# Down projection of a transformer block on one Trainium2 core: plain fp32 product or three split products

## The reference, cut to what matters

```python
c  = attention(x)                          # (8, 128, 512), summed over 8 groups of heads
s  = silu(c @ w_gate.T)                    # (8, 128, 1376)
s  = where(|s| is among the 688 smallest of its row, 0, s)
h  = s * (c @ w_up.T)
x1 = x + h @ w_down.T                      # the down product: 1376 -> 512
y  = x1 @ weight[adapter_ids[b]].T
out = x1 + (y @ unpack_int4(packed_w).T * scale_w + bias)
```

## Time and profile before

| | |
|---|---|
| median of 3 runs | 1397.92 us (1397.61 to 1399.25) |
| the profiled execution, its own time | 1399.51 us |
| its span (first to last instruction) | 1397.7 us |
| PE busy | 1376.4 us (98%) |
| DVE busy | 1181.5 us (85%) |
| ACT busy | 880.4 us (63%) |
| POOL busy | 795.0 us (57%) |
| granted TensorE clock, mean | 0.996 |

### The profile page before, as it was taken

One profiled execution on the slowest core, in us unless ns is written; L12 is line 12 of the kernel. 1 busy time (PEld: TensorE's weight loads), 2 busy tenths in 40 slices (PEclk: granted clock), 3 DMA queues, 4 the chain that ended last, 5 costly groups with the idle time before them and its releaser, 6 DMA issues.

```text
span 1397.7 us, 22868 instructions
## 1 busy us (share of the span) xinstructions
PE 1376.4 (98%) x7762; PEld 1159.6 (83%) x7762; DVE 1181.5 (85%) x2580; ACT 880.4 (63%) x2236; POOL 795.0 (57%) x832
## 2 busy tenths in 40 slices
PE   8899999999999999999999999999999999999998
PEld 6788888888888888888888888888888786667766
DVE  8989898989898989898989898999899887766662
ACT  6677676767676767676767676767777742222221
POOL 6867666666666666666676666666666500221211
PEclk9899999999999999999999999999999999999999
DMA  6111211111121112111211121212121203211121
GB/s 229 58 31 32 75 62 31 56 51 61 33 75 34 60 33 75 33 62 32 73 36 61 31 76 31 61 31 72 31 72 32 103 20 124 72 46 46 48 64 49
DMA packets 27408, 80.42 MB, mean 58 GB/s; under 512 B 9522, under 2 KB 10546, under 8 KB 23954
## 3 DMA queue, kind: packets, MB, share of 16 engines
q1 hardware_dynamic: 10898, 45.29, 9.2%
q0 software_dynamic: 16384, 33.59, 8.1%
HBM read 76.74 MB, written 2.10 MB: 56 GB/s over the span
## 4 chain that ended last, share of the span: by engine, by line
PE 89%; DVE 7%; issue 2%; ACT 2%; another core or an unknown queue 0%; POOL 0%; ACTq 0%; DVEq 0%
PE proj_ps L110 9%; PE proj_ps L112 9%; PE proj_ps L111 9%; PE turn_ps L750 9%; PE score_ps L112 5%; PE value_ps L110 5%; PE value_ps L111 5%; PE value_ps L112 5%; PE score_ps L111 5%; PE score_ps L110 5%; PE out_ps L932 5%; PE gu_ps L112 3%; PE gu_ps L110 3%; PE gu_ps L111 3%; PE turn_ps L712 2%; PE turn_ps L719 2%
## 5 line engine op out<-in xcount | busy, mean ns | idle before, releaser
L521 POOL DMA_INDIRECT kg<-kc,idx x256 | 260.7, 1018 | 277.9 <-issue 263.2
L1193 ACT ACTIVATE probs<-probs,shift,rstd 128x640 f32<-128x640 f32 x256 | 234.5, 918 | 137.3 <-DVE shift L1544 135.0
L531 POOL DMA_INDIRECT vg<-vc,idx x256 | 259.0, 1012 | 70.7 <-issue 70.7
L1580 DVE TENSOR_TENSOR pt_lo<-turn_ps,pt_hi 128x512 fp32r<-128x512 f32 x320 | 217.2, 686 | 44.6 <-ACT pt_hi L1199 39.1
L1555 DVE CUSTOM_DVE_ANT_0 probs<-score_ps,mask 128x640 f32<-128x640 f32 x256 | 208.7, 821 | 38.8 <-PE score_ps L112 35.6
L1199 ACT ACTIVATE pt_hi<-turn_ps 128x512 fp32r<-128x512 f32 x320 | 186.4, 593 | 86.6 <-PE turn_ps L750 77.4
L750 PE MATMUL turn_ps<-cst,probs 128*128 128x128 f32 x1280 | 192.7, 273 | 1.7 <-DVE qt_lo L1532 0.9
L110 PE MATMUL proj_ps<-w_hi,xt_parts 128*128 128x256 f32 (+1 forms) x500 | 190.4, 381 | 1.4 <-issue 1.4
L750 PEld LDWEIGHTS turn_ps<-cst,probs 128*128 128x128 f32 x1280 | 158.0, 141 | 28.5 <-DVE probs L1573 2.3
L112 PE MATMUL proj_ps<-w_hi,xt_parts 128*128 128x256 f32 (+1 forms) x500 | 169.6, 339 | 0.0
L111 PE MATMUL proj_ps<-w_lo,xt_parts 128*128 128x256 f32 (+1 forms) x500 | 168.6, 337 | 0.0
(11 more groups left out here) (214 smaller groups left out, 3213.5 us busy)
## 6 DMA issues: line engine op xcount, KB each, us to landing
w_raw<-wqkv SPq DMA_DIRECT2D x7, 1536.0 KB
wo_raw<-wo SPq DMA_DIRECT2D x8, 1024.0 KB
wa_sb<-wa SPq DMA_DIRECT2D x7, 1024.0 KB, 4.8
kg<-kc,idx POOLq DMA_INDIRECT x256
vg<-vc,idx POOLq DMA_INDIRECT x256
wg_raw<-wg SPq DMA_DIRECT2D x2, 1376.0 KB
wu_raw<-wu SPq DMA_DIRECT2D x1, 2752.0 KB
wd_sb<-wd SPq DMA_DIRECT2D x1, 2560.0 KB, 9.7
```

The source lines that it names most:

```text
L521: pool.indirect_dma_start(kg[:, b % 2, c, :], None, kc, bass.IndirectOffsetOnAxis(ap=idx[:, s // B % 2, b * NC + c:b * NC + c + 1], axis=0))\
L531: pool.indirect_dma_start(vg[:, b % 2, c, :], None, vc, bass.IndirectOffsetOnAxis(ap=idx[:, s // B % 2, b * NC + c:b * NC + c + 1], axis=0))\
L1193: act.activation(row, row, ACT.Exp, bias=shift[:, h:h + 1], scale=rstd[:, b % 2, h:h + 1], accum_out=sums[:, h:h + 1])\
L1580: dve.tensor_tensor(pt_lo[:, at, :], turn_ps[1 - j % 2][:, :], pt_hi[:, at, :].bitcast(F32), ALU.subtract).then_inc(p_lo_done[j], 1)
```

## The change

The down product becomes three split products. Its weights are split once for all tiles, and h is split in each tile:

- The down weights are loaded before the last step of phase 1 ends (all but the last chunk). ACT rounds them (`split_wd`, `split_wd_end`), DVE subtracts. The high parts of chunks 4 to 9 have a tile of their own (`wd_hi_own`); those of chunks 0 to 3 and of the last one lie in rows 0 to 4 of `acc` (`wd_hi_acc`), which are free once `front` has transposed those attention results. So tile 0 splits only chunks 4 to 9, tile 1 chunks 0 to 9, and tiles 2 to 7 all 11; the rest stays plain.
- ACT's `copy_h` now writes the rounded `ht_hi`, and DVE has a new operation `split_h(i, n)` for each job, which reads PSUM and `ht_hi` and writes `ht_lo`. PE waits for it through `h_ready`: `turn_h(i, 2)` may overwrite the PSUM of job 0 only after `split_h(i, 0)`, and the down product starts only after `split_h(i, 0)` and `split_h(i, 1)`.
- The selection works in place: one `m_sb` and one `w_sb` in place of two each, `junk` inside `w_sb`, and h written over s. So `magnitudes(i)` waits for h of tile i-1.
- `front` loses the copy `c_sb`: ACT rounds straight from PSUM, and the subtraction goes from POOL to DVE (`split_c`).
- The output is summed in `y` and not in `acc`; `copy_y` waits for the output transfer of the tile before.

```diff
+                    def split_down(i, c):
+                        return i >= (1 if c < 4 else 2 if c == NF - 1 else 0)
...
                     def turn_h(i, n):
...
-                            wait(pe, h_copied[0], i + 1)
+                            h_ready(i, 0)
...
+                    def h_ready(i, n):
+                        if n == 0:
+                            wait(pe, h_copied[0], 1)
+                        wait(pe, h_lo_done, 3 * i + n)
+                        if n == 2 and not split_down(i, NF - 1):
+                            wait(pe, h_copied[2], i + 1)
...
-                            last = pe.matmul(out_ps[:, :], ht[0:width, c, :], wd_sb[0:width, c, :],
-                                             start=(c == 0), stop=(c == NF - 1))
+                            if c == 0:
+                                h_ready(i, 0)
+                                h_ready(i, 1)
+                            elif c == 8:
+                                h_ready(i, 2)
...
+                            if split_down(i, c):
+                                last = product3(pe, to, (ht_his[t][0:width, c, :], ht_los[t][0:width, c, :]), (hi, lo),
+                                                first, end)
+                            else:
+                                last = pe.matmul(to, ht_raw[0:width, c, :], raw, start=first, stop=end)
...
                     def magnitudes(i):
                         wait(act, silu_done, i + 1)
-                        act.activation(m_sb[i % 2][:, :], s_sb[i % 2][:, :], ACT.Abs, accum_out=sum_m[i % 2][:, :])\
+                        wait(act, h_done, i)
+                        act.activation(m_sb[:, :], s_sb[i % 2][:, :], ACT.Abs, accum_out=sum_m[i % 2][:, :])\
                             .then_inc(abs_done, 1)
...
                     def pick(i):
-                        for guess in range(len(STEP_SIZES)):
-                            pick_guess(i, guess)
+                        pick_guess(i, 0)
+                        if i > 2 and i + 1 < B:
+                            split_c(i + 1)
+                        pick_guess(i, 1)
+                        pick_guess(i, 2)
+                        if i == 2:
+                            split_h(1, 0)
+                            split_wd(2)
+                            split_h(1, 1)
+                            split_h(1, 2)
+                        if i == 3:
+                            split_wd_end()
                         pick_near(i)
+                        if i > 2:
+                            split_h(i - 1, 0)
                         pick_edge(i)
+                        if i > 2:
+                            split_h(i - 1, 1)
+                            split_h(i - 1, 2)
...
                     pick_edge(0)
+                    split_wd(1)
                     drop_lower_half(0)
+                    split_wd(0)
+                    split_h(0, 1)
+                    split_h(0, 2)
                     unpack(1)
                     unpack_bias()
                     for i in range(1, B):
                         pick(i)
                         times_up(i)
+                        if i == 1:
+                            split_c(3)
                         drop_lower_half(i)
+                    for n in ALL_JOBS:
+                        split_h(B - 1, n)
```

More of the change, by code:

```diff
@@ new lines, in down_products @@
+                    def down_products(i, to, cols):
+                        t = own(i)
+                        for c in range(NF):
+                            width, first, end = FCH[c][1], c == 0, c == NF - 1
+                            raw, hi, lo = (w[0:width, cols] for w in wd_places(c))
+                            if c == 0:
[3 more added lines that the diff above has]
+                                h_ready(i, 2)
+                            if i == 0 and c in (4, 8):
+                                pe.wait_ge(wd_lo_done, 1 if c == 4 else 2)
+                            elif i == 1 and first:
+                                pe.wait_ge(wd_lo_done, 3)
+                            elif i == 2 and end:
+                                pe.wait_ge(wd_lo_done, 4)
+                            if split_down(i, c):
[3 more added lines that the diff above has]
+                                last = pe.matmul(to, ht_raw[0:width, c, :], raw, start=first, stop=end)
+                        last.then_inc(downed, 1)
@@ L1361, in copy_h @@
                         full = sum(width == P for _, width in job)
-                        last = act.activation(hts[t][:, c:c + full, :].rearrange("p c t -> p (c t)"),
+                        into = ht_his[t] if split_down(i, c) else ht_raw
+                        last = act.activation(into[:, c:c + full, :].rearrange("p c t -> p (c t)"),
                                               to[:, 0:full * P], ACT.Copy)
-                        for m in range(full, len(job)):
-                            width = job[m][1]
-                            last = act.activation(hts[t][0:width, c + m, :], to[0:width, m * P:(m + 1) * P], ACT.Copy)
+                        if full < len(job):
+                            width = job[full][1]
+                            into = ht_his[t] if split_down(i, c + full) else ht_raw
+                            last = act.activation(into[0:width, c + full, :], to[0:width, full * P:(full + 1) * P],
+                                                  ACT.Copy)
                         last.then_inc(h_copied[n], 1)
@@ new lines, in split_h @@
+                    def split_h(i, n):
+                        t = own(i)
+                        job, c, to = HT_JOBS[n], 4 * n, h_ps(i, n)
+                        dve.wait_ge(h_copied[n], i + 1)
+                        full = sum(width == P for _, width in job)
+                        last = dve.tensor_tensor(ht_los[t][:, c:c + full, :].rearrange("p c t -> p (c t)"),
+                                                 to[:, 0:full * P],
+                                                 ht_his[t][:, c:c + full, :].rearrange("p c t -> p (c t)").bitcast(F32),
+                                                 ALU.subtract)
+                        if full < len(job) and split_down(i, c + full):
+                            width = job[full][1]
+                            last = dve.tensor_tensor(ht_los[t][0:width, c + full, :],
+                                                     to[0:width, full * P:(full + 1) * P],
+                                                     ht_his[t][0:width, c + full, :].bitcast(F32), ALU.subtract)
+                        last.then_inc(h_lo_done, 1)
```

213 lines of the change are left out of this document (124 added, 89 removed).

## The result

| | median us | runs | ratio to before | clock |
|---|---|---|---|---|
| before | 1398.45 | 4, 1397.61 to 1399.25 | | 0.996 (profiled run) |
| changed | 1417.26 | 4, 1413.49 to 1418.07 | 1.0129 [1.0109, 1.0149] | 0.988 to 0.993 |

A forecast was written before the change was run, and what follows sets the result against it. PE, busy 98% of the span, was taken to set the pace. Waits of 22.2 and 0.7 us against 13.5 saved gave +9.5; five clock falls added 9.5: +19 on 1397.92, so 1417, range 1405 to 1423.

The forecast's parts named there:

- What the product saves: Down products in phase 2: 9.45 us plain, 7.62 split, so 1.83 less per full tile and 13.5 in all.
- The quarter: Down product: three products for four passes would save 2.36 of 9.45 us; the prediction went by the rows' 1.83 instead.
- When DVE is ready: Tile steps 4 to 6, T being the first up product's start: PE wants h's low part at T+14.1, starts at T+17.15.
- pick(2) starts: Tile step 2 on DVE: the pick starts near 1193.1 instead of 1189.6, behind subtractions and the magnitudes of tile 2.
- the working of step 2: Tile step 2: PE waits 3.3 us at the third group of transposes, down saves 1.65, net +1.65.
- The sum without the clock: All tile steps and the end part: 22.2 us of waits and 0.7 against 13.5 saved, +9.5 us.
- where -0.4 stood: Tile step 1: split_h(0, 1) delays the down product by 0.6 us against 1.0 saved.
- The step that failed: DVE's added split_c: taken as hidden behind POOL's addition in tile steps 4 to 6, costing nothing, at worst 0.65 us.
- The clock: New PE waits in phase 2: the clock falls to half behind five of six, +9.5 us; 64% for falls at most waits.
- a sign of being wrong: Phase 2: the prediction is wrong if the clock stays at 1.00 in spite of waits above 2.4 us.
- the 1.9 us taken from phase 1: Price of one clock fall: half of a 3.9 us slow stretch seen after a 2.43 us gap in phase 1.
- One row was misread: The page before the change: TensorE's granted clock read as full in all but two of 40 slices.

The follow-up runs named there:

- plain_down: The changed kernel with the old fp32 down product, no DVE split of weights or h, the rest of the change kept: 1401.20 us, ratio 1.0017.
- no_low: The changed kernel without DVE's subtractions of h; the third matmul of each chunk reads h's high part instead: 1389.11 us, ratio 0.9930.
- split_early: The changed kernel with DVE's subtractions for jobs 1 and 2 moved inside pick_edge in picks 3 to 7: 1396.99 us, ratio 0.9985.
- gate_twice: The changed kernel with useless repeated matmuls on PE before the down products of tile steps 3 to 7: 1410.60 us, ratio 1.0082.

## Why the prediction was right, and where it was not

**What the product saves: right.** Tile steps 4 to 6 go from 32.48 us (plain_down) to 30.65 (no_low), 1.83 each, as worked out from the pitch of 0.231 us. The quarter, an estimate from the four passes that the Trainium skill gives for true fp32 (FP8 and Floating Point Precision, TensorE Precision Notes), would have been 2.36; no run here shows it, and the measurement decides.

**When DVE is ready: right to 0.1 us in tile step 4 (T+17.12, T+17.15 forecast).** PE waits 2.84 us in steps 4 to 6 (3.05 forecast), 3.19 in step 3 (3.7 and 0.2), and 5.64 in step 7, of which 0.45 stood before as the wait for ACT; 5.2 more were forecast. In step 2 it waits 0.97 for POOL and 2.19 for `ht_lo`, together 3.16 (3.3). split_early shows that in steps 3 to 6 this is place alone, no_low that it is DVE's low part alone.

pick(2) starts at 1193.10, as forecast (1193.1), but that is luck: phase 1 of this execution was 0.9 us shorter than in the profile of before (silu(1) starts at 1154.72 and not at 1155.66). Counted from silu(1), pick(1) starts 1.8 us later (2.0 forecast), and pick(2) 4.4 (3.5 forecast). From the start of pick(1) to the end of h of tile 1 DVE takes 21.9 us and not 20.6, which the prediction had unchanged. Half of this is `split_c(3)` (0.68 us, its row stands under plain_c_late), which the working of step 2 leaves out. The other half is a meeting with POOL, in order of time on the two engines:

```profile
1177.33 2.31 DVE L1963 SCALAR_TENSOR_TENSOR w_sb<-m_sb,edge 128x1376 f32<-128x1376 f32 x1
```

```profile
1176.89 1.29 POOL L593 TENSOR_TENSOR x<-x,xn_sb 128x512 f32<-128x512 f32 x1 [44.39 <-ACT x L1417]
1178.27 2.52 POOL L598 TENSOR_TENSOR xn_sb<-x,bias 128x512 f32<-128x512 f32 x1
```

The pass takes 1.65 us elsewhere. Here POOL's addition was there first, and the pass became 0.66 longer; it then held POOL's next addition up.

**The sum without the clock: 9.5 forecast, about 10.5 measured.** From gate_twice less before, by the table, with the one fall of its last part (1.6) taken off: step 2 +2.24 (forecast 1.65), step 3 +2.40 (2.1), steps 4 to 6 +1.28 each (1.25), from silu(7) to the end +1.8 (2.4). The profiled execution of before had 0.8 us more span than the median of its runs (1397.7 against 1396.9), so what comes before silu(2) is nearer +0.2 than -0.6, where -0.4 stood. The terms that were too small are those up to step 2, by about 1.2 us. The step that failed is the one that took moved work at nothing: 1.3 us more on DVE between pick(1) and h of tile 1, as above, with PE waiting for what comes behind it. The prediction had seen that DVE and POOL hold each other up, but costed it and `split_c` only in tile step 4. (plain_down's +2.5 is not the price of this: in the changed kernel `split_c(3)` doesn't wait for ACT, and behind the 0.97 us for POOL PE would wait for `ht_lo` anyway.)

**The clock: right in kind, 9.5 forecast, about 8.3 measured.** 6.7 us are shown by the medians of gate_twice, 1.6 are the fall left in its profile. The Trainium skill (TensorE: Matmul & The Clock Gate, HAM oscillation) would have every portion behind a wait begin cold; the trace agrees in four of six waits of this execution, with two of 2.84 us at full clock and a third of 2.84 at half. The prediction had named a clock that stays full behind more than 2.4 us as a sign of being wrong, and twice it did. Each fall was also cheaper than the 1.9 us taken from phase 1: 1.6 in step 2 (36.26 against 34.70), 0.8 in step 3 (35.64 against 34.86), 1.3 in step 5 (35.01 against 33.72, where 35.5 to 36.5 was forecast), 1.3 in step 7 (8.95 us for the down product, 7.62 at full clock). In phase 1 PE had further gaps while it ran slowly, here products follow without one; that this makes the difference is not shown. These four are 5.0 us, in the shortest of the executions; those with clock 0.988 are some 4.6 us longer, about what two or three more falls and longer ones cost.

One row was misread: of the 40 slices of the earlier trace rows one, not two, is below 9. Nothing hangs on it.

So 1417.0 against 1417.26 is closer than the steps deserve: 1.0 us too little waiting and 1.2 us too much clock cancel. What carried the forecast was the order of time on two engines.

## What to carry to other kernels

When a product gets cheaper by a new operand, find the place of that operand in the queue of the engine that makes it, and compare its end with the time at which PE now wants it; 28 us of difference (1417.3 to 1389.1) hung on that, and 20 of them, the clock's part included, on moving two instructions ahead of search passes that PE was not waiting for. A buffer that is saved by working in place ties an engine's next pass to the reader of the last one, and holds what stands behind it in that queue; put what others wait for ahead of it. Remove a wait and read the trace again: the next one was there already, 3 us behind.

## What the runs showed of the hardware

- The clock behind an idle stretch of PE is not settled by its length alone: of three waits of 2.84 us at the same place of a tile step, two left it at 1.00 and one brought it to 0.51. A wait of 2.2 us in tile step 2 lowered it in one of four profiled executions.
- Useless matmuls in place of waits made the kernel 6.7 us faster (1417.26 to 1410.60), though no low part came earlier in its tile step. Before a single wait of 2 us they gave nothing (1394.12 and 1394.28; 1391.06 and 1391.54).
- A DVE pass over 128x1376 with both inputs in SBUF and an addition on POOL hold each other up, and the later one pays: POOL's took 2.35 us when the pass ran first, 1.30 when they didn't meet; the pass took 2.31 when POOL's ran first, 1.65 when nothing was in its way. A pass with one large input and an addition ran side by side in tile step 4 of the changed kernel, at 1.64 and 1.28 us.
